# Two tiles under one instruction in three output stages of a convolution block kernel on Trainium2

## The reference

```python
# layer 0 (z has 16 channels), g from the group-normalised image
x = x + sigmoid(h @ Wg + bg) * (_ln(z, ln2_g, ln2_b) @ Wz + bz)
# layer 1 (z has 32 channels), both factors from the normalised z
x = x + (zn @ po_w.T + po_b) * sigmoid(zn @ go_w.T + go_b)
# layer 2 (z has 64 channels), the gate was computed and stored earlier
x = x + (layer_norm(z) @ p_out_w.T) * gate
```

## Time and profile before

| what | value |
|---|---|
| time, three runs | 1638.24, 1638.46, 1645.11 us (median 1638.46) |
| profiled execution | 1645.97 us, its span 1644.2 us |
| granted PE clock over the span | 0.938 of full speed |
| busy share of the span | PE 87%, DVE 71%, ACT 64%, POOL 26% |
| POOL adds of the three stages (L1337) | 192 of 1274 ns, 241.3 us |
| sigmoids (L1312) | 128 in stages 0 and 1 |

### The profile page before, as it was taken

One profiled execution on the slowest core, in us unless ns is written; L12 is line 12 of the kernel. 1 busy time (PEld: TensorE's weight loads), 2 busy tenths in 40 slices (PEclk: granted clock), 3 DMA queues, 4 the chain that ended last, 5 costly groups with the idle time before them and its releaser, 6 DMA issues. The chain is left out here.

```text
span 1644.2 us, 26839 instructions
## 1 busy us (share of the span) xinstructions
PE 1424.4 (87%) x9117; PEld 739.0 (45%) x9117; DVE 1170.2 (71%) x2059; ACT 1051.8 (64%) x1845; POOL 428.3 (26%) x382
## 2 busy tenths in 40 slices
PE   6797797978697897899969999698989996995987
PEld 5435432222385342133428999222223335772444
DVE  5644687179699884389966777797169986998664
ACT  4675786844245786688855666554868884664555
POOL 5400297130000693310000000387130000001665
PEclk9898899989899898999989999799989998997999
DMA  8337310026776230079987887696038889996997
GB/s 343 116 153 284 126 52 1 1 79 197 238 274 257 90 103 1 1 276 339 351 304 296 305 304 259 243 349 252 1 154 346 345 343 343 419 419 232 384 401 305
DMA packets 151671, 381.66 MB, mean 232 GB/s; under 512 B 14704, under 2 KB 14960, under 8 KB 151408
## 3 DMA queue, kind: packets, MB, share of 16 engines
q1 hardware_dynamic: 139152, 356.63, 58.9%
q10 hardware_dynamic: 12384, 23.31, 3.8%
HBM read 191.14 MB, written 188.74 MB: 231 GB/s over the span
## 5 line engine op out<-in xcount | busy, mean ns | idle before, releaser
L1337 POOL TENSOR_TENSOR xT<-xT,work 128x512 f32<-128x512 f32 x192 | 241.3, 1274 | 677.4 <-DVE work L1382 675.2
L1014 PE MATMUL bank<-work 128*128 128x256 f32 x1408 | 336.4, 387 | 20.7 <-DVE work L1084 11.3
L745 ACT ACTIVATE work<-bank,bias 128x512 f32<-128x512 f32 x448 | 286.0, 685 | 95.8 <-PE bank L644 42.0
L1014 PEld LDWEIGHTS bank<-work 128*128 128x128 f32 x1408 | 263.0, 196 | 68.0 <-issue 14.8
L644 PE MATMUL bank<-work,w 64*64 64x512 f32 x2048 | 257.4, 605 | 6.0 <-ACT work L741 6.0
L817 DVE SCALAR_TENSOR_TENSOR work<-bank,bias,work 128x512 f32<-128x512 f32 x320 | 236.6, 748 | 30.9 <-PE bank L644 23.3
L1044 ACT COPY work<-bank 128x512 f32<-128x512 f32 x176 | 103.1, 586 | 154.2 <-PE bank L1014 152.7
L1382 DVE SCALAR_TENSOR_TENSOR work<-bank,bias,work 128x512 f32<-128x512 f32 x192 | 141.7, 747 | 39.9 <-ACT work L1312 19.5
L1526 POOL TENSOR_TENSOR xT<-xT,work 128x512 f32<-128x512 f32 x64 | 80.2, 1274 | 340.5 <-ACT work L1496 340.3
L1110 DVE TENSOR_TENSOR work<-work 128x512 f32<-128x512 f32 x176 | 121.6, 691 | 58.3 <-ACT work L1044 57.1
L644 PEld LDWEIGHTS bank<-work,w 64*64 64x64 f32 x2048 | 85.4, 134 | 139.5 <-DVE work L817 79.9
(11 more groups left out here) (146 smaller groups left out, 2074.4 us busy)
## 6 DMA issues: line engine op xcount, KB each, us to landing
hidden_rows<-work SPq DMA_DIRECT2D x128, 512.0 KB, 4.0
work<-hidden_rows SPq DMA_DIRECT2D x120, 512.0 KB, 6.5
products<-work SPq DMA_DIRECT2D x88, 512.0 KB, 3.9
work<-products SPq DMA_DIRECT2D x88, 512.0 KB, 5.3
work<-gate_rows SPq DMA_DIRECT2D x64, 512.0 KB, 5.9
work<-hidden SPq DMA_DIRECT2D x40, 512.0 KB, 6.1
work<-in_x SPq DMA_DIRECT2D x32, 512.0 KB, 4.8
gate_rows<-work SPq DMA_DIRECT2D x32, 512.0 KB, 3.3
```

The source lines that it names most:

```text
L745: nc.scalar.activation(result(t, column), GB[n % len(GB)][:, :], ACT.Sigmoid, bias=bias(name)).then_inc(gate_sb, 1)
L1014: mm = pe.matmul(ZB[c % 2][:, r * N:r * N + N], a[:, kk, rows_of(r, c)], x[:, kk, :], start=(kk == 0), stop=(kk == 1))
L1337: pool.tensor_tensor(columns(t), columns(t), term[:, t % RING, :], ALU.add).then_inc(x_sb, 1)
```

## The change

In the three stages an instruction of ACT, DVE or POOL works on two tiles (a *duo*, numbered p = 0 to 31; 1024 columns) at once where it worked on one: the normalisation on the two banks FAC, the sigmoid on the two banks GB, the gating on two neighbouring banks of OB, the addition, and the square sums. The eight banks become one PSUM tensor, so that an instruction can run over neighbours. Matmuls still write one bank each. With the instructions the semaphore counts change: the gate products of a duo wait for the sigmoid of the whole duo before, factors come for two units at once and wait for the normalisation of the two units before, and an output product waits for the gating two duos back. On PE the factors of the next two units come behind the first unit of the current two (stages 0 and 1) or ahead of it (stage 2); DVE still runs the normalisation of the next two units ahead of the first gating of the current two. The tiles counted on DVE go from 21 to 16 in stage 0 and from 16 to 12 in stage 1.

```diff
-        self.counted_on_vector = {0: list(range(3, NT, 3)), 1: list(range(3, NT, 4)), 2: []}
+        duos = {0: range(3, NT // 2, 4), 1: range(4, NT // 2, 5), 2: []}
+        self.counted_on_vector = {layer: [t for p in duos[layer] for t in (2 * p, 2 * p + 1)] for layer in duos}
...
-        self.bank = [ctx.enter_context(nc.psum_tensor(f"bank{n}", [P, T], F32)) for n in range(8)]
+        self.banks = ctx.enter_context(nc.psum_tensor("banks", [P, 8, T], F32))
+        self.bank = [self.banks[:, n, :] for n in range(8)]
...
-    UNITS, IN, RING, LAG = NT // nq, 3, 4, 4
+    UNITS, IN, LAG = NT // nq, 3, 2
+    DUOS = NT // 2
...
-    term, at = core.area([RING, T], 0)
+    term, at = core.area([2, 2, T], 0)
     z, at = core.area([IN, 2, T], 4 * T)
-    gate, at = core.area([IN, 2, T] if stored_gate else [RING, T], at)
+    gate, at = core.area([IN if stored_gate else 2, 2, T], at)
     spread, at = core.area([4, T], at, BF16)
-    squares, at = core.area([2, T], at)
+    squares, at = core.area([2, 2, T], at)
...
+    def duo(p):
+
+        first, second = tile(2 * p), tile(2 * p + 1)
+        return xT[:, :].rearrange("p (n x) -> p n x", x=T)[:, first:second + 1:second - first, :]
...
-                    sp.wait_ge(term_sb, 2 * (i - IN + 1))
+                    sp.wait_ge(term_sb, i - IN + 1)
...
-            def factor(s):
-                if s >= UNITS:
+            def factors(v):
+                if v >= UNITS // 2:
                     return
...
+                at_least(pe, zn_sb, v)
+                for s in (2 * v, 2 * v + 1):
...
+                    core.spread_factors(pe, nq, FAC[s % 2], spread[:, x, :], k).then_inc(fac_mm, 1)
 
             def gate_product(t, weights, moving):
-                at_least(pe, gate_sb, t - 1)
+                at_least(pe, gate_sb, t // 2)
                 pe.matmul(GB[t % 2][:, :], weights, moving, start=True, stop=True).then_inc(gate_mm, 1)
 
             def out_product(t, moving):
-                at_least(pe, term_sb, t - 3)
+                at_least(pe, term_sb, t // 2 - 1)
...
-                pe.wait_ge(zn_sb, s + 1)
+                pe.wait_ge(zn_sb, s // 2 + 1)
...
-            factor(0)
-            for s in range(UNITS):
-                factor(s + 1)
-                unit(s)
+            factors(0)
+            for v in range(UNITS // 2):
+                if nq == 1:
+                    factors(v + 1)
+                unit(2 * v)
+                if nq > 1:
+                    factors(v + 1)
+                unit(2 * v + 1)
 
         @block.scalar
         def _(act):
-            def gated(t):
-                act.wait_ge(gate_mm, t + 1)
-                at_least(act, term_sb, t - RING + 1)
-                nc.scalar.activation(gate[:, t % RING, :], GB[t % 2][:, :], ACT.Sigmoid, bias=gate_b).then_inc(gate_sb, 1)
-
-            def square_sum(t):
-                if t in counts_on_vector:
+            def gated(p):
+                act.wait_ge(gate_mm, 2 * p + 2)
+                at_least(act, term_sb, p - 1)
+                nc.scalar.activation(gate[:, p % 2, :, :], core.banks[:, 2:4, :], ACT.Sigmoid, bias=gate_b).then_inc(gate_sb, 1)
+
+            def square_sums(p):
+                if p in counts_on_vector:
                     return
-                act.wait_ge(x_sb, t + 1)
...
-                nc.scalar.activation(squares[:, n % 2, :], columns(t), ACT.Square, bias=core.shift,
-                                     accum_out=core.tile_sums[:, 1, t:t + 1]).then_inc(sq_sb, 1)
+                nc.scalar.activation(squares[:, n % 2, :, :], duo(p), ACT.Square, bias=core.shift,
+                                     accum_out=core.tile_sums[:, 1, p:p + 1]).then_inc(sq_sb, 1)
 
             roots.on_scalar(act)
...
+            for p in range(DUOS + LAG):
+                if p < DUOS and not stored_gate:
+                    gated(p)
+                if p >= LAG:
+                    square_sums(p - LAG)
 
         @block.gpsimd
         def _(pool):
-            for t in range(NT):
-                pool.wait_ge(term_sb, t + 1)
-                pool.tensor_tensor(columns(t), columns(t), term[:, t % RING, :], ALU.add).then_inc(x_sb, 1)
+            for p in range(DUOS):
+                pool.wait_ge(term_sb, p + 1)
+                pool.tensor_tensor(duo(p), duo(p), term[:, p % 2, :, :], ALU.add).then_inc(x_sb, 1)
 
...
-            def normed(s):
-                if s >= UNITS:
+            def statistics(p):
+                if p in counts_on_vector:
+                    dve.wait_ge(x_sb, p + 1)
+                    for t in (2 * p, 2 * p + 1):
+                        n = core.counted_on_vector[layer].index(t)
+                        dve.bn_stats(core.tile_stats[:, 6 * n:6 * n + 6], columns(t)).then_inc(counted, 1)
+
+            def normed(v):
+                if v >= UNITS // 2:
                     return
-                zt = z[:, s // 2 % IN, s % 2, :]
-                if s % 2 == 0:
-                    dve.wait_ge(landed[s // 2 % IN], 16 * (s // 2 // IN) + 16)
-                dve.wait_ge(fac_mm, s + 1)
-                dve.tensor_tensor(zt, FAC[s % 2][:, :], zt, ALU.mult).then_inc(zn_sb, 1)
-
-            def gate_of(t):
+                zt = z[:, v % IN, :, :]
+                dve.wait_ge(landed[v % IN], 16 * (v // IN) + 16)
+                dve.wait_ge(fac_mm, 2 * v + 2)
+                dve.tensor_tensor(zt, core.banks[:, 0:2, :], zt, ALU.mult).then_inc(zn_sb, 1)
+
+            def gate_of(p):
                 if not stored_gate:
-                    dve.wait_ge(gate_sb, t + 1)
-                    return gate[:, t % RING, :]
-                if t % 2 == 0:
-                    dve.wait_ge(gates_in[t // 2 % IN], 16 * (t // 2 // IN) + 16)
-                return gate[:, t // 2 % IN, t % 2, :]
+                    dve.wait_ge(gate_sb, p + 1)
+                    return gate[:, p % 2, :, :]
+                dve.wait_ge(gates_in[p % IN], 16 * (p // IN) + 16)
+                return gate[:, p % IN, :, :]
 
             roots.on_vector(dve)
             dve.memset(core.tile_sums[:, 1, :], 0.0).then_inc(counted, 1)
             normed(0)
-            for s in range(UNITS):
-                normed(s + 1)
-                for t in range(nq * s, nq * s + nq):
-                    gt = gate_of(t)
-                    dve.wait_ge(out_mm, t + 1)
-                    at_least(dve, x_sb, t - RING + 1)
-                    dve.scalar_tensor_tensor(out=term[:, t % RING, :], in0=OB[t % 4][:, :], scalar=out_b, in1=gt,
-                                             op0=ALU.add, op1=ALU.mult,
-                                             accum_out=core.tile_sums[:, 0, t:t + 1]).then_inc(term_sb, 1)
-                    if t == 2:
-                        first_shift()
-                    if t >= 3:
-                        statistics(t - 3)
-            for t in range(NT - 3, NT):
-                statistics(t)
+            for p in range(DUOS):
+                if p % nq == 0:
+                    normed(p // nq + 1)
+                gt = gate_of(p)
+                dve.wait_ge(out_mm, 2 * p + 2)
+                at_least(dve, x_sb, p - 1)
+                dve.scalar_tensor_tensor(out=term[:, p % 2, :, :], in0=core.banks[:, 4 + 2 * (p % 2):6 + 2 * (p % 2), :],
+                                         scalar=out_b, in1=gt, op0=ALU.add, op1=ALU.mult,
+                                         accum_out=core.tile_sums[:, 0, p:p + 1]).then_inc(term_sb, 1)
+                if p == 1:
+                    first_shift()
+                if p >= 2:
+                    statistics(p - 2)
+            for p in range(DUOS - 2, DUOS):
+                statistics(p)
```

More of the change, by code:

```diff
@@ L1222, in finish @@
     stored_gate = layer == 2
-    counts_on_vector = core.counted_on_vector[layer]
+    counts_on_vector = sorted({t // 2 for t in core.counted_on_vector[layer]})
     FAC, GB, OB = bank[0:2], bank[2:4], bank[4:8]
-    term, at = core.area([RING, T], 0)
+    term, at = core.area([2, 2, T], 0)
     z, at = core.area([IN, 2, T], 4 * T)
-    gate, at = core.area([IN, 2, T] if stored_gate else [RING, T], at)
+    gate, at = core.area([IN if stored_gate else 2, 2, T], at)
     spread, at = core.area([4, T], at, BF16)
-    squares, at = core.area([2, T], at)
+    squares, at = core.area([2, 2, T], at)
     w = lambda name: core.w[:, SLOT[name], :]
@@ L1314, in square_sum @@
-            def square_sum(t):
-                if t in counts_on_vector:
+            def gated(p):
[4 more added lines that the diff above has]
+                if p in counts_on_vector:
                     return
-                act.wait_ge(x_sb, t + 1)
-                if t == 0:
+                act.wait_ge(x_sb, p + 1)
+                if p == 0:
@@ L1319, in square_sum @@
                     act.wait_ge(shifted, 3)
                     act.wait_ge(counted, 1)
-                n = t - sum(c < t for c in counts_on_vector)
+                n = p - sum(c < p for c in counts_on_vector)
```

(47 more changed lines are left out.)

10 lines of the change are left out of this document (4 added, 6 removed).

## The result

The changed kernel is slower: 1677.24 us in the median of four runs (1669.61 to 1679.57) against 1641.47 for the kernel before (1638.24 to 1645.11). The medians differ by 35.8 us. The ratio of the runs is recorded as 1.0201, 95% interval 1.017 to 1.0232, so +33 us (28 to 38).

What follows compares the result with a forecast made beforehand. PE, ACT and POOL were taken as tied together in stage 0, with DMA full in stage 2. Stages of +24.4, -2 and +4 sum to +26.4 us on a median of 1638.46: 1665 us, forecast's own range 1658 to 1674.

Steps and rivals of the forecast that it cites:

- second rival: Whole kernel: longer landings (5.7 us in stage 2) and a lower PE clock; +42 us, 1680 us; chance 14%.
- The gate turn: Stage 0: two gate products and their shared sigmoid can't overlap, a closed loop of 3.18 us a duo against 2.65.
- The late factors: Stage 0: normalisation waits for factors behind the second gate turn, delaying the fourth duo's output products; 0.45 us a round.
- half of 1.07: Stage 0: PE time taken for one duo's output products, where four tiles take 1.07 us, within the late-factor delay.
- The PE clock: Stage 0: PE only about 70% busy is granted a lower clock; +2 us, bounds 0 and 4.
- Stage 0 as a sum: Stage 0: turn, late factors, longer tail and lower clock together cost +24.4 us.
- The tail: Stage 0, last sigmoid to end of last statistics: 6.2 us against 4.2, +2.0 us.
- Stage 1: Turn of 2.56 us a duo against 2.70, less longer tail and late factors: -2 us, bounds -5 and +2.
- Stage 2: Load round over three duos, landing 5.0 us, gives 2.96 us a duo against 2.89; with tail +4 us, bounds -5 and +15.
- All else: Outside the three stages the kernel runs as before; 0 us.
- the gate turn alone: Rival: only the turn costs time; factors, clock and landings cost nothing more; +13.5 us, 1652 us; chance 20%.
- POOL as the bound: Rival: all three stages run at the add's pace of 2.38 us a duo; -29 us, 1609 us; chance 3%.

Runs made afterwards that it cites:

- runs 3: Kernel before, single tiles, only two waits changed: gate products wait for all earlier pairs' sigmoids, sigmoids for both products of their pair; 1696.36 us, ratio 1.0320.
- run 5: Kernel before with those pair waits, and on ACT both sigmoids of a pair ahead of its two square sums; 1661.62 us, ratio 1.0133.
- run 6: Changed kernel with a sigmoid per tile, gate products waiting two tiles back, and factors ahead of the first unit; 1649.75 us, ratio 1.0058.
- run 2: Changed kernel with the next two units' factors ahead of the first unit on PE in all three stages; 1670.46 us, ratio 1.0162.
- run 1: Changed kernel with a sigmoid per tile again and gate products waiting for the sigmoid two tiles back; 1674.21 us, ratio 1.0181.
- run 4: Changed kernel with four buffers instead of three for z and the gates in stage 2; 1661.57 us, ratio 1.0106.

## Why the prediction was right

The forecast was slower by 26 us, the measured ratio says 33 (28 to 38), and 28.5 us of the profiled difference lie in the three stages. The direction and the mechanism hold. The size is less close than the stage table makes it look: the median of 1677.24 us lies above the forecast's own 1658 to 1674 and nearer to the second rival's 1680, and within stage 0 errors cancel.

- **The gate turn**: right, 3.19 us against 3.18, and the runs show it by itself (runs 3 and 5: the waits without the instructions; run 6 against run 2: the two banks in rotation again, 10.29 us a round against 12.76). The pace before was misread: 5.30 us is one unit's time, but 58 adds in 75 us are 2.59 us for two tiles and not 2.65. So the turn cost 32 x 0.60 = 19.2 us, where the sum has 17.0.
- **The late factors**: right in place, too small. I put 0.45 us a round, 13.2 us in all; it was 0.9 and 13.64. Seven rounds were to have it, 3.2 us; six had it, 5.3 us. The term that was mis-sized is "half of 1.07" for the output products of one duo: the eight passes of four tiles run side by side in 1.07 us, and half of them alone take the same, 246.95 - 245.89 = 1.06 us.
- **What I did not see**: that the way over the factors is a loop of its own, 12.4 us long. I had it only as an addition to the turn, which was enough for the sum of the changed kernel, but the expectation for run 1 rested on it and failed.
- **The PE clock**: wrong. I added 2 us for a less busy PE; the granted clock of stage 0 stayed at 1.00.
- **Stage 0 as a sum**: near (25.2 against 24.4), in part by luck. The turn and the delay were 2.2 and 2.1 us too small, the clock 2 us too large, and the measured parts (19.2, 5.3 and 2.0) make 26.5, 1.3 more than the stage.
- **The tail**: right, 6.2 against 4.2 us.
- **Stage 1**: right in size (-2.6 against -2). With the factors early (run 2) it is 1.9 us shorter still. From the first gating to the last it gains 7.3 us, more than the forecast 4.5; what follows the last gating costs 2.8 (2.0 forecast) and the start 2.0, which the sum didn't have. That the gain comes from larger instructions, as the prediction's turn has it, is not shown: run 5 has it with single tiles and the sigmoids of a pair side by side.
- **Stage 2**: right in kind. The round over three duos was landing-bound, 3.06 us against 2.96, with a landing of 5.4 where I took 5.0; one more buffer removes it (run 4). The sum is off in its parts: from the first to the last gating it grew by 0.7 us only (2.3 forecast), the tail by 2.0 (1.6), and the start by 3.3, a term that the sum doesn't have. Four profiles of this form have 105.6 to 110.2 us and three of the old one 96.5 to 99.6, so the loss of one pair of profiles, 5.9 us, is the least of what they allow.
- **All else**: 5.1 us of the profiled difference lie where no instruction changed, 4.1 of them ahead of stage 0. In the ten profiles this rest runs from 1359.7 to 1369.4 us, with the changed kernel's at the top, so I read it as scatter. What causes it is open, and so is whether it explains that the interval of the ratio (28 us at least) barely takes in the stages' 28.5.
- **The rivals**: the gate turn alone (+13.5) is refuted by run 2, POOL as the bound by POOL's 71%. Even with the turn opened and the factors early (run 6) a duo takes 10.29 / 4 = 2.57 us with PE busy 69.84 of 70 us, so stage 0 is back at PE's own pace and not at POOL's. The rival of longer landings and a lower clock (+42) had the 0.9 us a round right and the clock wrong; its landing of 5.7 us was 5.4.

The Trainium skill (Perfetto Trace Analysis, Matmuls) asks for rotation through PSUM banks so that reading one out (evacuation) overlaps the next group. The trace agrees: the same two GB banks rotated and not rotated are 92.06 and 110.31 us (runs 6 and 2).

## What to carry to other kernels

When two buffers are merged under one instruction, they are one buffer: ask for the closed loop that this makes (producer, merged consumer, producer) and compare its length with the engines' own work before counting the saved fixed costs. Merge only where a second pair of buffers stays free (advice that follows from the loop; no run here had a second pair), and look for what else the merged instruction waits for and pull it ahead in the producer's order. With two loops of like length either edit alone shows only a part: here 5.3 and 4.8 us where both together brought 23.1. A merged consumer also wants its loads earlier, so count the look-ahead again, and it starts later and ends later in every stage, so count the start as well as the tail.

## What the runs showed of the hardware

- Slopes over other operations of the same engine predicted three unseen shapes within 2% (1.28, 1.21 and 1.11 us; measured 1.279, 1.225 and 1.114): an instruction over two neighbouring PSUM banks costs what its elements cost, with no extra for the second bank to be seen. The add on POOL saves 0.19 us for two tiles in one (2 x 1.274 - 2.362).
- A half-filled set of row tiles takes PE as long as a full one: from their first weight load to the next gate product's, four passes of 32 rows took 1.06 us (changed kernel, 245.89 to 246.95) and eight 1.07 (kernel before, 246.05 to 247.12).
- PE's granted clock was 1.00 in stage 0 of the changed kernel with PE 83% busy, and 0.88 in three rounds of run 1 with PE 93% busy. In the first of those rounds the weight loads of gate passes stand 0.85 us apart (242.31, 243.16), in the round before 0.43 (229.74, 230.17); that is the lower level (1.2 of 2.4 GHz) for part of the round. What PE did before does not tell them apart: in the rounds at 1.00 it was 92% busy (11.41 of 12.41 us), and it waited the same 0.96 us for DVE in them (before 227.04) as in the round in which the clock fell (before 239.45). Why it fell is open.
